# A Fourier mixing layer rebuilt inside a fused fp32 kernel: tiles by row quarter, a ring of weights, four column tiles

## The chip, the cores and the metric

One core of a Trainium2 chip runs the whole program. The metric is the device time of one execution in microseconds. The profile is of one such execution; all times in it count from the first instruction.

## What is computed

The input x has shape (8, 32, 32, 192) in fp32. Two layers follow one another; the change is in the first and in where things lie.

```python
def layer0(x, w1, b1, ...):
    xn = layernorm(x, norm1_w, norm1_b)
    xf = rfft2(xn, axes=(1, 2), norm='ortho')        # 32 x 17 bins
    xf = xf.reshape(B, h, w // 2 + 1, 8, 24)
    o1 = einsum('bhwni,hwnio->bhwno', xf, w1c) + b1c # own weights in every bin
    o1 = complex(relu(o1.real), relu(o1.imag))
    xs = irfft2(o1, s=(h, w), axes=(1, 2), norm='ortho')
    xm = layernorm(xs, norm2_w, norm2_b)
    return xs + x + gelu(xm @ mlp_w1 + mlp_b1) @ mlp_w2 + mlp_b2
def layer1(x, ...):                                  # not touched but for buffers
    h = gated_scan(layernorm(x), 8 steps)
    x = x + h
    return x + gelu(layernorm(x) @ mlp_w1 + mlp_b1) @ mlp_w2 + mlp_b2
```

## The kernel before

`build` (L202) runs `fourier` (L216), `inverse_rows` (L703), `mlp` (L818) for the first layer, then `gated_scan` (L1137) and `mlp` again. Each function opens a block with one program per engine; the programs wait on semaphores, and the order on each engine is the order in which it is written. SP, ACT and POOL also issue DMAs, each in its own program: while an engine issues, what is behind waits.

**Row stage (in `fourier`).** X (64 tiles of 128 tokens by 192 channels; a tile is four image rows) is loaded by POOL, one image of 8 tiles at a time (L357). Per image DVE takes the statistics (L483, L489, with an epsilon added at L491), ACT the root, and DVE (L506) and ACT (L409) normalise four tiles each into `row_bufs`. PE multiplies by the row DFT (L620), ACT copies PSUM out (L419), and SP stores the result into the DRAM tensor `rows_spectrum`, four DMAs per image (L304). POOL meanwhile clears S and Y with memsets (L365, L366), loads small vectors, and when all images are normalised adds the second MLP bias b2 to all 64 tiles of X (L375). ACT's program also issues the weights of the first two units between images (`load_weights`, L282/L283).

**Unit loop (in `fourier`).** The 17 column bins are taken in 8 groups g of two bins; each group has two halves s of 96 channels: 16 units, and two units more for the last (Nyquist) bin, which fill one bin each. Of a group, `d2` is loaded (SP, L315), and PE applies the DFT down the columns with the data as the loaded operand (L642; L652 for the Nyquist part that comes with group 0). DVE scales by the layernorm gain into `xh` (L535; for the group 0 the constant term is added at L544), ACT's or SP's queue expands `xh` by DMA into S, which holds each of the four 24-channel blocks in its own place with zeros elsewhere (`expand`, L291). The products (L667) take S as the loaded operand, 64 columns with a stride of 256 bytes, and the weights Wt as the streamed one, 48 wide, in two column tiles of the array; a matmul is two records in the profile. ACT copies cross terms (L449, L451), DVE adds (L564), transposes (L571) and applies the relu (L575) into Z. PE inverts the columns of a group (L677), DVE copies into `d3` (L584, L608), and POOL stores `d3` to the DRAM tensor `rows_mixed` (L382, L387).

**Inverse rows and the first MLP.** `inverse_rows` loads `rows_mixed` again (SP, L734), multiplies (L751), copies to XS (ACT, L766) and takes statistics (L785, L790), while ACT and POOL split the MLP weights into high and low parts (`high_parts`, `low_parts`, L806 to L815). In `mlp`, DVE scales XS into xn (L999), eight operations per group of four tiles, while POOL adds XS to X, 16 operations of four tiles (L905), signalled by the semaphore `biased`. In the second `mlp` POOL instead adds b2 tile by tile (L900).

## Time and profile before

| | us |
|---|---|
| median of 3 runs (1276.23 to 1278.8) | 1276.27 |
| the profiled execution | 1273.96 |
| its span, first to last instruction | 1272.6 |
| PE / DVE / ACT / POOL busy in it | 1114.9 / 879.9 / 665.2 / 347.9 |
| mean granted TensorE clock | 0.889 |

The span lies 1.4 us under the execution's own time, and that one 2.3 us under the median of the runs. Busy shares are averages over stages that have different limits: the Fourier layer takes the first 392 us, its MLP, the scan and the second MLP the rest.

### The profile page before, as it was taken

The page shows a single profiled execution, that of the slowest core. Times are in us where ns is not written, and L with a number is a line of the kernel's source. Part 1 is how long each engine was busy: PE and PEld are TensorE (multiplying, and loading weights), DVE is VectorE, ACT ScalarE, POOL GpSimd, SP SyncE. Part 2 cuts the span into 40 slices and gives each one's busy share as a digit, 9 for nine tenths or more (in the row PEclk, how much of TensorE's full clock was granted, in tenths as well). Part 3 has the DMA queues.
Part 4 walks back from the last instruction along what each step waited for, and adds up shares of the span by engine and source line. Part 5 has one row for each costly group of instructions (what it writes and reads, how often), then busy time and mean ns, then how long its engine had stood idle before and what let it go on. Part 6 is the DMA issues. An engine that isn't in the chain of part 4 may idle for free. (4 is left out here: it accounts for less than half of the span.)

```text
span 1272.6 us, 22506 instructions
## 1 busy us (share of the span) xinstructions
PE 1114.9 (88%) x7072; PEld 905.8 (71%) x7072; DVE 879.9 (69%) x2183; ACT 665.2 (52%) x1299; POOL 347.9 (27%) x351
## 2 busy tenths in 40 slices
PE   2634799999754899999989999999999889999998
PEld 1224788888522788888876776767767668889997
DVE  6626465555437788887776877969969867766665
ACT  2421334344133565666667757756664346676555
POOL 4564011001008200000013743734716621111110
PEclk9665677878567899999999999999999879999999
DMA  8653999996172000000010000000000000001001
GB/s 245 146 133 76 178 174 201 198 182 122 31 202 65 1 1 0 0 0 0 0 44 1 1 1 1 1 1 1 1 1 1 1 1 25 25 26 36 25 25 37
DMA packets 153073, 70.22 MB, mean 55 GB/s; under 512 B 117968, under 2 KB 145392, under 8 KB 153008
## 3 DMA queue, kind: packets, MB, share of 16 engines
q1 hardware_dynamic: 129208, 47.38, 18.2%
q10 hardware_dynamic: 19232, 9.18, 3.8%
q0 software_dynamic: 4576, 12.93, 3.5%
q8 instruction: 33, 0.54, 0.2%
q14 instruction: 24, 0.20, 0.1%
HBM read 43.91 MB, written 18.87 MB: 49 GB/s over the span
## 5 line engine op out<-in xcount | busy, mean ns | idle before, releaser
L1129 PE MATMUL L_conv_ps<-w2hl,L_conv_hhi 128*128 128x384 f32 x768 | 229.0, 366 | 1.3 <-DVE X L1025 1.3
L939 ACT ACTIVATE L_conv_hf<-L_conv_ps,L_conv_b 128x512 f32<-128x512 f32 x192 | 132.1, 688 | 175.0 <-PE L_conv_ps L1110 170.2
L1129 PE MATMUL L_conv_ps<-w2hl,L_conv_hlo 128*128 128x192 f32 x768 | 188.6, 252 | 0.0
L1015 DVE TENSOR_TENSOR L_conv_hlo<-L_conv_hf,L_conv_hhi 128x512 fp32r<-128x512 f32 x192 | 129.4, 688 | 84.5 <-ACT L_conv_hhi L948 81.5
L1521 PE MATMUL sc_ps<-sc_hi,wh 128*128 128x512 f32 (+1 forms) x440 | 161.0, 438 | 3.4 <-ACT sc_prod L1303 3.2
L1129 PEld LDWEIGHTS L_conv_ps<-w2hl,L_conv_hhi 128*128 128x128 f32 x768 | 144.7, 188 | 4.6 <-DVE X L1025 2.1
L1521 PE MATMUL sc_ps<-sc_hi,wl 128*128 128x512 f32 (+1 forms) x440 | 147.8, 392 | 0.0
L1129 PEld LDWEIGHTS L_conv_ps<-w2hl,L_conv_hlo 128*128 128x128 f32 x768 | 146.6, 191 | 0.0
L449 ACT ACTIVATE cross<-psF 32x192 f32<-32x192 f32 x136 | 43.8, 322 | 175.1 <-PE psF L667 165.9
L1376 DVE TENSOR_TENSOR sc_prod<-sc_ps,sc_gate 128x512 f32<-128x512 f32 x168 | 110.2, 680 | 15.1 <-PE sc_ps L1521 15.1
L948 ACT ACTIVATE L_conv_hhi<-L_conv_hf 128x512 fp32r<-128x512 f32 x192 | 116.3, 622 | 0.0
L1521 PEld LDWEIGHTS sc_ps<-sc_hi,wh 128*128 128x128 f32 (+1 forms) x440 | 70.7, 187 | 55.2 <-issue 40.0
L1521 PE MATMUL sc_ps<-sc_lo,wh 128*128 128x512 f32 (+1 forms) x440 | 107.6, 393 | 0.0
L1243 POOL TENSOR_TENSOR sc_lo<-sc_prod,sc_hi 128x512 fp32r<-128x512 f32 x64 | 95.2, 1511 | 22.7 <-ACT sc_hi L1319 22.7
L900 POOL TENSOR_TENSOR X<-X,L_conv_b 128x192 f32 x64 | 36.8, 606 | 193.8 <-DVE L_conv_xn L999 193.8
L642 PE MATMUL psF<-fwd_h,d 128*96 128x128 f32 x256 | 56.3, 410 | 36.9 <-DVE dc L552 18.7
L564 DVE TENSOR_TENSOR Y<-psF,cross 128x192 f32<-128x192 f32 (+1 forms) x72 | 25.6, 356 | 87.1 <-ACT cross L451 87.1
L1110 PE MATMUL L_conv_ps<-L_conv_thi,w1h 128*128 128x512 f32 x192 | 77.8, 405 | 7.0 <-ACT L_conv_hf L939 4.2
L1521 PEld LDWEIGHTS sc_ps<-sc_lo,wh 128*128 128x128 f32 (+1 forms) x440 | 71.2, 188 | 15.2
L1110 PE MATMUL L_conv_ps<-L_conv_tst,w1h 128*128 128x512 f32 x192 | 77.2, 402 | 2.5 <-DVE L_conv_tst L1010 2.5
L642 PEld LDWEIGHTS psF<-fwd_h,d 128*96 128x96 f32 x256 | 51.7, 269 | 38.9 <-DVE dc L552 18.9
L1521 PEld LDWEIGHTS sc_ps<-sc_hi,wl 128*128 128x128 f32 (+1 forms) x440 | 71.0, 188 | 10.3
(139 smaller groups left out, 2313.8 us busy)
## 6 DMA issues: line engine op xcount, KB each, us to landing
row_bufs<-in_L_conv_w SPq DMA_DIRECT2D x16, 576.0 KB
Wt<-in_L_conv_w SPq DMA_DIRECT2D x14, 576.0 KB
X<-in_x POOLq DMA_DIRECT2D x8, 768.0 KB, 6.0
rows_spectrum<-row_bufs SPq DMA_DIRECT2D x32, 192.0 KB, 3.3
d<-rows_spectrum SPq DMA_DIRECT2D x8, 768.0 KB, 4.9
S<-xh ACTq DMA_DIRECT2D x64, 96.0 KB
rows_mixed<-d POOLq DMA_DIRECT2D x32, 192.0 KB, 5.9
d<-rows_mixed SPq DMA_DIRECT2D x8, 768.0 KB, 8.5
```

The costliest lines, as they stand in the source:

```text
L449: nc.scalar.activation(cross[j % 2][re:re + H], v[im:im + H, :, :, 1], ACT.Copy, scale=-1.0).then_inc(crossed, 1)
L564: nc.vector.tensor_tensor(Y[0:n, 8 * j:8 * j + 8, :], v[0:n, :, :, 0], cross[j % 2][0:n], ALU.add).then_inc(summed, 1)
L642: mm = pe.matmul(ps[0:HALF, 4 + q, P * b:P * b + P], d2[:, 4 * q + b, HALF * s:HALF * s + HALF], table, start=True, stop=True)
L900: nc.gpsimd.tensor_tensor(X[:, GT * i + k, :], X[:, GT * i + k, :], b2[:, :], ALU.add).then_inc(biased, 1)
L939: nc.scalar.activation(hf[:, m % 3, :], ps[:, RB + m % 2, :], gelu, bias=b1[:, m:m + 1]).then_inc(act1, 1)
L948: nc.scalar.activation(hhi[:, m, :], hf[:, m % 3, :], ACT.Copy).then_inc(h_hi, 1)
L1015: nc.vector.tensor_tensor(hlo[:, m, :], hf[:, m % 3, :], hhi[:, m, :].bitcast(F32), ALU.subtract).then_inc(h_lo, 1)
L1110: mm = pe.matmul(ps[:, RB + m % 2, :], w, x[:, :], start=(q == 0), stop=(q == 4))
L1129: mm = pe.matmul(o, x, w, start=(m == 0 and n == 0), stop=(m == MT - 1 and n == 1), skip_group_check=True)
L1243: nc.gpsimd.tensor_tensor(lo[c][:, j, :], value(c, s)[:, j, :], hi[c][:, j, :].bitcast(F32), ALU.subtract).then_inc(q["h_lo"], 1)
L1376: step_product = nc.vector.tensor_tensor(prod[c][:, j, :], ps[:, 3 * c + j, :], gate[c][:, j, :], ALU.mult)
L1521: return pe.matmul(out, ww[rows, cols], x[rows, j, :], start=first, stop=last, skip_group_check=True)
```

## The change

- Tiles are numbered by row quarter: eight slabs, each with one group of four rows of each of the 8 images, in place of eight images. Slabs of x, normalised x and row spectra live in XS, which is now there from the start. X is not filled in the row stage.
- `rows_spectrum` is laid out so that a slab is stored by one DMA of rows of 6144 bytes, on POOL (L366). The memsets on POOL and the 64 additions there go; the additions now stand in the loop of POOL in the first `mlp` (L837), ahead of the wide addition (L842), with a wait on the new semaphore `based` between them.
- The weights go through a ring of four units in X's place, all issued by SP, from the third slab on. After the last four units SP loads x once more into X (`again`), and the MLP weights.
- A unit has both bins of one half, and the Nyquist bin with both halves is one unit (`None`): 17 units. In the products (L621) the weights are the loaded operand, 24 columns in each of four column tiles, and S streams, 64 wide at a stride of 256 bytes; real and imaginary weights accumulate, so S has three parts (-im, re, im).
- S is written from PSUM directly: for every part and channel block one scaling by gain times mask, 12 on DVE (first four images) and 12 on ACT (other four). `xh`, the expansion DMAs, the cross copies and the sums go.
- ACT applies the relu from PSUM (two of 512 elements a unit) into Y, DVE transposes 1024 elements into Z.
- The inverse column transform (L637) goes in halves between the units. `d3` is copied by DVE and ACT and written into XS by DMAs within SBUF (POOL, L374, 8 per group, 96 KB each); `rows_mixed` and its loads are gone, and `inverse_rows` works in place.
- The scan's buffers move into XS, and the output is stored slab by slab.

The core of the diff:

```diff
-        F1 = nc.dram_tensor("rows_spectrum", [W, H, B, C], F32, kind="Internal").ap()
-        F2 = nc.dram_tensor("rows_mixed", [B, H, W, C], F32, kind="Internal").ap()
+        F1 = nc.dram_tensor("rows_spectrum", [P, TPB, B * C], F32, kind="Internal").ap()
...
+        Wt = [X[0:HALF + NH, NT // RING * r:NT // RING * (r + 1), :].rearrange("p a c -> p (a c)").rearrange(
+            "p (k h o r) -> p k h o r", k=2, h=H, o=BS) for r in range(RING)]
...
+        units = [(0, 0), (0, 1), None] + [(g, s) for g in range(1, NG) for s in range(2)]
...
         @block.sync
+            sp.wait_ge(x_in[XT - 1], 16)
+            for u in range(UNITS):
+                r = u % RING
+                if u >= RING:
+                    sp.wait_ge(mixed, 2 * (u - RING + 1))
+                for k in range(2):
+                    s, at = (k, WF - 1) if units[u] is None else (units[u][1], 2 * units[u][0] + k)
+                    into = Wt[r][:, k].rearrange("p h o r -> p h (o r)")
+                    sp.dma_start(into[0:HALF], w_v[s, at]).then_inc(w_in[r], 16)
+                    sp.dma_start(into[HALF:HALF + NH], b_v[s, at]).then_inc(w_in[r], 16)
...
+            for u in range(UNITS - RING, UNITS):
+                sp.wait_ge(mixed, 2 * (u + 1))
...
+                again(u)
...
         @block.gpsimd
-            for s in range(2):
-                nc.gpsimd.memset(S[s][:, :, :], 0.0).then_inc(zeroed, 1)
-            nc.gpsimd.memset(Y[:, :, :], 0.0).then_inc(zeroed, 1)
...
-            with pool.Fori(0, B) as b:
-                for k in range(TPB):
-                    nc.gpsimd.tensor_tensor(X[:, b * TPB + k, :], X[:, b * TPB + k, :], sh.b2["L0_conv_"][:, :],
-                                            ALU.add).then_inc(x_biased, 1)
...
+            for k in range(TPB):
+                if k + XT < TPB:
+                    load(k + XT)
+                pool.wait_ge(d1_done, 4 * (k + 1))
+                pool.dma_start(F1[:, k, :], d1[k % 2].rearrange("p b c -> p (b c)")).then_inc(f1_out[k % 2], 16)
...
+            for g in range(NG):
+                pool.wait_ge(d3_v, 2 * (g + 1))
+                pool.wait_ge(d3_a, 2 * (g + 1))
+                for k in range(TPB):
+                    pool.dma_start(XS[g:P:NG, B * k:B * (k + 1), :].rearrange("p b c -> p (b c)"),
+                                   d3[g % 2][k:P:TPB, :]).then_inc(sh.rows_in[g % 2][k], 16)
...
         @block.vector
+            def spread(u):
+                dve.wait_ge(hdft, u + 1)
+                if u >= 2:
+                    dve.wait_ge(mixed, 2 * (u - 1))
+                v = ps[0:HALF, col_bank(u), :].rearrange("p (b r f) -> p r b f", b=B // 2, r=2)
+                for cut, of in slots(u):
+                    for part, n in itertools.product(range(3), range(NH)):
+                        scale = (ngm if part == 0 else gm)[:, of, n:n + 1]
+                        nc.vector.tensor_scalar(S[u % 2][0:HALF, part, n, 0:B // 2, cut], v[:, int(part != 1), :, cut], scale,
+                                                None, ALU.mult).then_inc(spread_v, 1)
...
         @block.tensor
-            def products(u, s, g, p, times, bins=2):
-                for j in range(4):
-                    passed(pe, summed, 4 * (u - 1) + j + 1)
-                    for hl in range(8):
-                        for k in range(bins):
-                            h = 8 * j + hl
-                            mm = pe.matmul(ps[2 * H * k:2 * H * k + 2 * H, j, 48 * hl:48 * hl + 48],
-                                           S[s][:, :, k * H + h], Wt[p][s][:, k, h, :], start=True, stop=True)
+            def products(u):
+                r = u % RING
+                pe.wait_ge(w_in[r], 64 * (u // RING + 1))
+                spread_done(u)
+                for hl in range(H // 2):
+                    q, col = hl // 8, 2 * NH * B * (hl % 8)
+                    if hl % 8 == 0 and u >= 2:
+                        pe.wait_ge(relu, 2 * (u - 2) + q + 1)
+                    for part in range(2):
+                        for j in range(4):
+                            k, h = j // 2, H // 2 * (j % 2) + hl
+                            mm = pe.matmul(ps[H * j:H * j + BS, 2 * (u % 2) + q, col:col + 2 * NH * B],
+                                           Wt[r][:, k, h, :, part],
+                                           S[u % 2][:, 1 - part:3 - part, :, :, k * H + h].rearrange("p a n b -> p (a n b)"),
+                                           start=(part == 0), stop=(part == 1), skip_group_check=True)
...
+                for k in range(GT):
+                    nc.gpsimd.tensor_tensor(X[:, GT * i + k, :], X[:, GT * i + k, :], b2[:, :],
+                                            ALU.add).then_inc(biased if XS is None else based, 1)
+                if XS is not None:
+                    pool.wait_ge(based, GT * (i + 1))
                     tiles = bass.ds(GT * i, GT)
                     nc.gpsimd.tensor_tensor(X[:, tiles, :], X[:, tiles, :], XS[:, tiles, :], ALU.add).then_inc(biased, GT)
```

How the order moves on PE in the unit loop. Before, units run in a loop over pairs of groups, with the products of one unit in four quarters, then the columns of the unit two ahead, then in every second unit a whole inverse:

```order
L667 MATMUL psF<-Wt,S 64x48 x16
L78 REGISTER_ALU
L667 MATMUL psF<-Wt,S 64x48 x16
L78 REGISTER_ALU
L667 MATMUL psF<-Wt,S 64x48 x16
L78 REGISTER_ALU
L667 MATMUL psF<-Wt,S 64x48 x16
L633 ISA
L640 ISA
L642 MATMUL psF<-fwd_h,d 96x128 x4
L640 REGISTER_ALU
L642 MATMUL psF<-fwd_h,d 96x128 x4
```

Of the changed kernel, the same place, written out without a loop (`spectrum` is S, `X` holds the ring of weights):

```order
L621 MATMUL psF<-spectrum,X 24x64 x128
L604 MATMUL psF<-fwd_h,d 96x128 x8
L637 MATMUL psF<-Z,inv_h 128x384 x2
L621 MATMUL psF<-spectrum,X 24x64 x128
L604 MATMUL psF<-fwd_h,d 96x128 x8
L637 MATMUL psF<-Z,inv_h 128x384 x2
```

A unit has 128 product matmuls where it had 64, and two inverse matmuls stand behind every unit where four stood behind every second one.

On POOL at the start of the first MLP, before:

```order
L891 MEMSET raw 128x320
L892 MEMSET raw 128x256
L907 UNCONDITIONAL_BRANCH
L907 ISA
L905 TENSOR_TENSOR X<-X,XS 128x768
```

And in the changed kernel, where the last rows are the loop's body:

```order
L829 MEMSET spectrum 128x320
L830 MEMSET spectrum 128x256
L848 UNCONDITIONAL_BRANCH
L848 ISA
L837 TENSOR_TENSOR X<-X,L_conv_b 128x192
L837 ISA
L837 TENSOR_TENSOR X<-X,L_conv_b 128x192
L837 ISA
L837 TENSOR_TENSOR X<-X,L_conv_b 128x192
L837 ISA
L837 TENSOR_TENSOR X<-X,L_conv_b 128x192
L840 ISA
```

The four bias additions now stand ahead of each wide addition, and the ISA row of L840 is the wait on `based`.

## Rows read from the trace of the kernel before

**Rows 1.** The page: engines (busy us, share, instructions), and a DMA issue (median us).

```profile
PE 1114.9 (88%) x7072; PEld 905.8 (71%) x7072; DVE 879.9 (69%) x2183; ACT 665.2 (52%) x1299; POOL 347.9 (27%) x351
...
rows_mixed<-d POOLq DMA_DIRECT2D x32, 192.0 KB, 5.9
```

**Rows 2.** Stretches of core 0: engine busy us (instructions), PEclk, DMA share, GB/s.

```profile
77.00:118.00 41.00, 11.24 (x68) 11.00 (x68) 24.18 (x15) 0.00 (x0) 33.19 (x61) 0.58 0.22 55
118.00:342.00 224.00, 207.16 (x2464) 187.40 (x2462) 114.95 (x193) 86.91 (x271) 21.83 (x31) 0.72 0.92 163
```

**Rows 3.** Timeline, row stage: start us, us, engine, line, operation, [idle before <-releaser].

```profile
15.90 6.25 PE L620 MATMUL psF<-row_bufs,fwd_w 128*128 128x384 f32 x12 [15.90 <-DVE row_bufs L506]
...
26.75 6.19 DVE L491 TENSOR_SCALAR mvb<-mvb 128x8 f32<-128x8 f32 x1
...
37.81 1.86 ACT L409 ACTIVATE row_bufs<-X,shift,rs 128x192 f32 x4 [13.08 <-issue]
...
61.22 0.32 ACTq L282 DMA_DIRECT2D Wt<-in_L_conv_w  x1
...
68.25 1.86 ACT L409 ACTIVATE row_bufs<-X,shift,rs 128x192 f32<-128x192 f32 x4 [6.68 <-issue]
```

**Rows 4.** Timeline between the last row copy and the first products.

```profile
76.71 2.69 SPq L304 DMA_DIRECT2D rows_spectrum<-row_bufs  x4
...
85.47 6.68 POOL L375 TENSOR_TENSOR X<-X,L_conv_b 128x192 f32 x12
...
87.07 3.70 PE L642 MATMUL psF<-fwd_h,d 128*96 128x128 f32 x16 [10.91 <-DMA d<-rows_spectrum]
...
91.78 18.75 DVE L544 TENSOR_SCALAR xh<-xh,dc 96x8 f32<-96x8 f32 x1
...
117.81 7.35 PE L667 MATMUL psF<-Wt,S 100*64 100x48 f32 x128 [0.97 <-DVE x L549]
```

**Rows 5.** Timeline, the unit loop: two starts of products a group apart, one single-tile unit.

```profile
212.29 7.37 PE L667 MATMUL psF<-row_bufs,S 100*64 100x48 f32 x128
...
236.75 0.43 PE L667 MATMUL psF<-Wt,S 100*64 100x48 f32 x4
...
327.49 14.39 PE L667 MATMUL psF<-Wt,S 100*64 100x48 f32 x128
```

**Rows 6.** Products line L667 alone, in two stretches at different granted clock.

```profile
119.30:124.30 5.00, 5.00 (x96) 5.00 (x94) 0.50 1.10 248
...
223.00:228.00 5.00, 5.00 (x96) 5.00 (x92) 1.00 0.94 235
```

**Rows 7.** Groups by shape in 118 to 342 us: count, busy us, mean ns, idle before.

```profile
L642 PE MATMUL psF<-fwd_h,d 128*96 128x128 f32 x224 | 48.9, 408 | 7.3 <-DMA d<-rows_spectrum 7.3
...
L449 ACT ACTIVATE cross<-psF 32x192 f32<-32x192 f32 x136 | 43.8, 322 | 175.1 <-PE psF L667 165.9 <-issue 7.0
...
L571 DVE STREAM_TRANSPOSE Yt<-Y 128x768 f32<-128x768 f32 x17 | 35.2, 2073 | 0.1
L677 PE MATMUL psF<-Z,inv_h 128*128 128x384 f32 x64 | 29.4, 593 | 9.4 <-DVE Z L575 4.8 <-DVE d L584 4.6
L535 DVE TENSOR_SCALAR xh<-psF,gamma 96x256 f32<-96x256 f32 x56 | 24.0, 475 | 12.6 <-PE psF L642 12.5
```

**Rows 8.** Timeline, the last products and the inverse row transform.

```profile
341.91 0.32 ACT L449 ACTIVATE cross<-psF 32x192 f32<-32x192 f32 x1 [1.10 <-PE psF L667]
...
366.00 1.65 PE L751 MATMUL psI<-d,inv_w 128*128 128x384 f32 x2 [14.69 <-DMA d<-rows_mixed]
```

**Rows 9.** Timeline, the start of the first MLP: POOL and DVE.

```profile
392.70 29.35 POOL L905 TENSOR_TENSOR X<-X,XS  x16
...
393.22 13.70 DVE L999 TENSOR_SCALAR L_conv_xn<-XS,mv,L_conv_rs 128x192 f32<-128x192 f32 x8
...
413.20 9.71 DVE L999 TENSOR_SCALAR L_conv_xn<-XS,mv,L_conv_rs 128x192 f32<-128x192 f32 x8
...
431.95 2.15 DVE L999 TENSOR_SCALAR L_conv_xn<-XS,mv,L_conv_rs 128x192 f32<-128x192 f32 x8
```

More of the change, by code:

```diff
@@ new lines, in fourier, with operations, slots @@
+        UNITS = len(units)
+        last_of = [2] + [2 * g + 2 for g in range(1, NG)]
+        def operations(u, engine):
+            halves = 2 if units[u] is None else 1
+            return 3 * NH * halves + (NH if u < 2 and engine == "v" else 0)
+        spread_by = {e: list(itertools.accumulate(operations(u, e) for u in range(UNITS))) for e in "va"}
+        def slots(u):
+            if units[u] is None:
+                return [(slice(H * s, H * (s + 1)), s) for s in range(2)]
+            return [(slice(0, 2 * H), units[u][1])]
@@ L610, in _ @@
+            inverse_out(NG - 2, 1) if last_of[NG - 2] + 2 >= UNITS else None
+            for half in range(2):
+                inverse_out(NG - 1, half)
         @block.tensor
@@ L671, in inverse @@
-            def inverse(g, rows=P, width=P):
-                pe.wait_ge(relu, 2 * (g + 1))
-                z = Z[0:rows].rearrange("p b s c -> p (b s c)")
-                for j in range(4):
-                    passed(pe, d3_done, 4 * g + j - 1)
-                    pe.matmul(ps[0:width, 6 + j % 2, 0:384], inv_h[0:rows, 0:width], z[:, 384 * j:384 * j + 384],
-                              start=True, stop=True).then_inc(inv_done, 1)
-            def group(g, p, times):
-                for s in range(2):
-                    products(2 * g + s, s, g, p, times)
-                    if not (isinstance(g, int) and g == NG - 1):
-                        columns(2 * (g + 1) + s, s, g + 1)
-                    if s == 0 and not (isinstance(g, int) and g == 0):
-                        inverse(g - 1)
@@ L689, in _, with spread_done @@
[L689 to L703 removed]
+            def spread_done(u):
+                pe.wait_ge(spread_v, spread_by["v"][u])
+                pe.wait_ge(spread_a, spread_by["a"][u])
@@ new lines, in _ @@
+            pe.wait_ge(d1_done, 4 * TPB)
+            pe.wait_ge(consts, 16 * 3)
+            columns(0)
+            columns(1)
+            for u in range(UNITS):
+                products(u)
+                if u + 2 < UNITS:
+                    columns(u + 2)
+                for g in range(NG):
+                    if u == last_of[g] + 1:
+                        inverse(g, 0)
+                    elif u == last_of[g] + 2:
+                        inverse(g, 1)
+            inverse(NG - 2, 1) if last_of[NG - 2] + 2 >= UNITS else None
@@ L706, in inverse_rows @@
+            for half in range(2):
+                inverse(NG - 1, half)
+def inverse_rows(nc, t, sh, XS):
     mv = sh.mv
```

673 lines of the change are left out of this document (293 added, 380 removed).

## The prediction

> **What bounds the kernel now.** I read the engine table of the page first: TensorE (PE) is busy 88% of the span [rows 1], but from 437 us on it runs without a hole, and the change leaves that part alone. So I cut the first 437 us into stages with the busy times by stretch [rows 2]. Two things stand out. From 77 to 118 us PE does 11.2 us of work in 41, and POOL is the engine that is full (33.2). From 118 to 342 us PE is busy 207 of 224 us at a mean granted clock of 0.72, with the DMA engines at 0.92 beside it. Then I read the timeline of each stage for what ended last. In the row stage two waits stop everything: the DVE row of 6.19 us beside POOL's memsets, and ACT's two idle times of 13.08 and 6.68 us ended by "issue", during which ACT only issues weight loads [rows 3]. Between the stages the columns start 10.4 us after the last row copy, through two DMA legs, and then one tiny DVE addition lasts 18.75 us while POOL runs its additions X += b2 at 0.557 us each (6.68/12) [rows 4]. In the loop one group of two units takes 24.46 us (212.29 to 236.75), so 12.2 per unit, of which products take 7.37 [rows 5]. After it the inverse row transform waits 14.69 us for a store and a load [rows 8], and the first MLP starts slowly beside POOL [rows 9].
>
> **Row stage and hand-over.** The weight loads leave ACT's queue for SP's, and the POOL memsets go (one DVE memset of PSUM instead). An undisturbed stretch is 37.81 to 61.22 us, four images, 5.85 each, 5.95 with the steps between [rows 3]. First matmul at 15.9 as before, eight tiles: 15.9 + 8 x 5.95 = 63.5, last copy about 64 instead of 76.7. Four units of weights are now loaded in that stage beside X and F1; SP's other work is small, and POOL's queue carries X loads and F1 stores, each of the latter waiting for its tile, which holds back only loads three tiles ahead. I cost that at nothing, and bound it by 0 and 8 us (if the DMA engines are as full as in the loop, 0.92 and more). To the columns 11 us (10.4 before): 75. Columns 3.7. Then DVE and ACT each scale 12 pieces of 96x256 from PSUM. DVE's nearest row is 0.475 us for the same shape [rows 7], a little less back to back, 12 x 0.43 = 5.2; ACT's nearest is 0.322 for 192 elements [rows 7], so 12 x 0.4 = 4.8 beside it. Four additions of the DC term and hand-overs take 1.8. First products at 75 + 3.7 + 5.2 + 1.8 = **85.8 against 117.8: minus 32.0**. The largest part is the removed wait of 18.75 behind POOL and the expansion DMAs behind it.
>
> **Unit loop.** A unit now has 128 matmuls instead of 64, in four column tiles of 24 columns instead of two of 64, and the 64-wide operand with a stride of 256 B streams instead of being loaded. What does one cost? In two tiles 128 records take 7.37 us. The single-bin unit uses one tile and takes 14.39 for 128 records, 112 ns each [rows 5]; so each tile goes at 112 ns per record and two do not disturb one another. The same unit runs at one speed at granted clock 0.50 and 1.00 (96 records in 5.00 us in both) [rows 6], so the pace is not the array's but of reading or issuing. My value: four tiles at 112 ns side by side, 256/4 x 112 = 7.17, plus 0.2 for waits: P = 7.36, as before. Bounds: below, 6.4, if loading 24 columns instead of 64 shortens a record by some 15%; above, 14.4, if only two tiles advance at once. I take the value in the row's own manner because both pieces of a record stay about as large together. 17 x 7.36 = 125. Columns cost 48.9/14 = 3.5 per unit, 15 of them: 52. Inverse: 29.4/64 x 4 = 1.85 per half, 14 halves: 26 [rows 7]. The additions of group 0 and the Nyquist columns: 4. Sum 207, so the last products end at 85.8 + 207 = **293 against 342: 49 us ahead, 17 more than at the start**. The old loop had 18 units, of which two were single-tile at 14.39; they are one unit of 7.36 now, which saves 21.4, and the rest (group 0 inside the loop, one more pass of columns) gives some 4 back.
>
> What hides in it: DVE per unit transposes 1024 elements instead of 768 (2.07 x 4/3 = 2.76), scales 12 pieces (4.8) and copies (0.5): 8.1 us of 12.4. ACT: two rectifications of 512 elements (about 0.7 each), 12 scalings (4.8), a copy: 6.7. The next columns need the previous spread, which is through 8.3 us after its products end, while the next-but-one column pass comes 12.6 after. The expansion DMAs go, so DMA (0.92 with them) falls. None of them becomes late unless a scaling takes over 0.75 us.
>
> PE instruction overhead: the Trainium skill, "TensorEngine Tiling (Array Packing)", section Instruction Overhead, says a matmul has some 60 cycles of its own and that no tiling should be taken from a side that is already small. By it, as an estimate, 256 records of 25 to 50 ns, issued one by one, would take 6.4 to 12.8 us, so it speaks for the slow side of this term; the trace, with 57.5 ns per record in two tiles and 112 in one, does not show the floor.
>
> **Tail.** Before, 24.1 us from the last products to the inverse rows: turn, inverse, and 14.69 of two DMA legs [rows 8]. Now one leg on the same POOL queue, 5.9 us from issue to landing [rows 1], 6.3 with its first issue: 24.1 - 8.4 = 15.7. The inverse rows keep their 26 us (same matmuls, same copies, in place). MLP start at 293 + 41.7 = **334.7 against 392.1: minus 57.4**. The reload of X (8 x 768 KB) begins four units before the end and its last quarter lands some 10 us after the products, under the 42 us; cover gone, it would cost the difference.
>
> **First MLP.** The 64 additions X += b2 don't go away; they now stand in POOL's loop there. Before, 16 additions of 768 elements take 29.35 us, and DVE's scalings crawl beside them: 8 in 13.70, 8 in 9.71, the next 8 free in 2.15 [rows 9]. So one DVE operation passes per POOL operation of 1.8. Now an iteration is 4 x 0.557 + 0.2 + 1.83 = 4.3 us, the burst 16 x 4.3 = 69 instead of 29. How many DVE operations pass per iteration? The row of 18.75 us [rows 4] says that between additions which follow without a wait none gets in (18.75/0.557, some 34 in a row). A gap comes where POOL waits for its four additions, and after the wide one: two. So 8 scalings take 17.4, three groups 52 instead of 25.6; a little of it is covered: **plus 24**. Bounds: minus 5, if one passes after each addition (three groups in 21), and plus 47, if only one gets in per iteration (two groups in 70, the third in 2.2).
>
> The Trainium skill, "SBUF — State Buffer", section Who interferes with whom, calls this an exclusive lock on the port pair shared by DVE and GpSimd, held for one instruction; by it DVE would get in at the end of each addition and the term would be minus 5 instead of plus 24. The row of 18.75 us through 34 additions speaks against it.
>
> **Sum.** 1273.96 (the profiled execution) - 57.4 + 24 = 1240.6. The median of the runs before is 2.3 above the profiled execution; added, **1243 us** against 1276.27, 33 us or 2.6% faster. A change under 0.2% (2.5 us) is what a measurement of this kernel can't tell from none.
>
> **Rivals.**
> (A) *Slower: the four tiles advance in pairs only*, or the strided stream takes twice what the strided load took. The place is the products of every unit, the price 17 x (14.4 - 7.36) = 120 us: 1243 + 120 = 1363. It decides from P = 9.3 on (33/17 above 7.36), where the whole gain is gone. For it: the clock-independent 57.5 ns per record [rows 6], which fits a limit shared by both tiles as well as one of each; against it, the 112 ns of a lone tile [rows 5]. Chance 0.17.
> (B) *A floor of issuing or reading near 36 ns per record*, between the two: P = 9.2, 17 x 1.84 = 31 more: 1274, about the time before. For it the page named above; nothing in the rows. Chance 0.11, split over the bound on both sides.
> (C) *POOL's additions let DVE in each time*: term minus 5, so 1214. Chance 0.08, for the rule of the lock, against it the 18.75 us. Its opposite, one slot per iteration, gives 1266 and lies within the forecast's range.
> (D) *Products faster*, P = 6.4: 17 x 0.96 = 16 less, 1227. The loaded side shrinks from 64 to 24 columns. Chance 0.12.
> (E) *The change doesn't do what it says*: the spread from PSUM costs over 0.75 us a piece, and DVE paces the unit at 14 us: 17 x 1.7 = 29 more, 1272. Against it 0.475 for the same shape. Chance 0.04.
> Forecast: 0.48, its own range 1228 to 1266.
>
> **How the numbers follow.** Below 1212 I leave 0.04, above 1308 0.16 (rival A in full). Range **1212 to 1308**. Faster: forecast 0.48 + C 0.08 + D 0.12 + 0.02 of E and 0.04 of B = 0.74, less 0.03 for the row stage's and MLP's upper bounds falling together: 0.71. Same: 0.04. Slower: 0.25.
>
> **What would show it.** In the changed profile: first products at 86 us; 256 records of products in 7.4 us per unit (this is the step that could be wrong by most; over 9.3 and the kernel is not faster); unit period 12.4; last products at 293; MLP start at 335; the first scalings of that MLP in 17 us per eight, and POOL's burst of 69 us. A first-products time over 94 would say that the four units of weights crowd the row stage. A DVE row of 17 us anywhere before the loop would say a POOL operation was left there.

## The result and the profile after

| | before | changed |
|---|---|---|
| median of 4 runs each, us | 1276.25 (1274.5 to 1278.8) | 1227.14 (1223.21 to 1229.31) |
| the profiled execution / its span | 1273.96 / 1272.6 | 1229.31 / 1227.1 |
| first products / last products end | 117.8 / 342 | 90.0 / 303.0 |
| inverse rows start / first MLP starts | 366.0 / 392.1 | 323.8 / 347.4 |

The changed kernel takes 0.961 of the time before (95% interval 0.9581 to 0.964): 3.9%, 49 us faster. The profiled execution of the changed kernel was its longest of the four, 2.2 us over the median.

The two profiled spans differ by 45.5 us. By the table, 27.8 of them lie before the first products, 11 between these and the end of the last products, 3.3 from there to the inverse rows, 2.5 in the inverse rows and 1.2 in the first MLP.

From the page of the changed kernel, the engines and the queue that loads program code (packets, MB, share of 16 DMA engines; before it had 33 packets and 0.54 MB):

```profile
PE 1092.4 (89%) x9256; PEld 885.9 (72%) x9256; DVE 854.0 (70%) x2230; ACT 697.0 (57%) x1293; POOL 365.5 (30%) x388
...
q8 instruction: 55, 0.90, 0.3%
```

Busy time by stretch (length, then PE, PEld, DVE, ACT, POOL busy with counts, granted clock, DMA share, GB/s), to hold against [rows 2]:

```profile
77.00:90.00 13.00, 5.92 (x36) 5.77 (x37) 5.55 (x17) 5.60 (x16) 9.18 (x17) 0.63 0.48 138
90.00:303.00 213.00, 192.82 (x4677) 173.54 (x4677) 103.89 (x237) 110.81 (x247) 22.82 (x48) 0.87 0.82 151
303.00:324.00 21.00, 5.06 (x14) 2.38 (x14) 2.80 (x4) 2.50 (x4) 7.58 (x16) 0.74 0.63 150
324.00:347.00 23.00, 22.48 (x64) 12.80 (x64) 17.99 (x110) 17.20 (x36) 6.17 (x3) 0.93 0.01 1
347.00:420.00 73.00, 56.24 (x278) 46.78 (x279) 66.81 (x132) 33.63 (x59) 70.25 (x75) 0.88 0.04 9
```

The empty stretch before the loop is 13 us of columns and spread instead of 41. In the loop (90 to 303) PE is busy 193 of 213 us, where it was 207 of 224, at a mean granted clock of 0.87 instead of 0.72.

The timeline around it. DVE waits for a slab of x, the last row copies, the first columns, the first unit of products; before, the last row copy began at 76.2 and the products at 117.81 [rows 4]:

```profile
17.60 0.36 DVE L479 BATCH_NORM_STATS2 st<-XS 128x6 f32<-128x192 f32 x1 [5.26 <-issue]
...
67.14 1.60 ACT L402 ACTIVATE XS<-psF 128x384 f32<-128x384 f32 x4
...
80.60 5.90 PE L604 MATMUL psF<-fwd_h,d 128*96 128x128 f32 x32 [12.40 <-DMA d<-rows_spectrum]
...
89.97 7.43 PE L621 MATMUL psF<-spectrum,X 100*24 100x64 f32 x256 [3.48 <-ACT spectrum L431]
```

Groups by shape in the loop (count | busy us, mean ns | idle before, releaser), which answer to [rows 7]:

```profile
L621 PE MATMUL psF<-spectrum,X 100*24 100x64 f32 x4352 | 129.5, 290 | 23.7 <-issue 20.2 <-ACT spectrum L431 3.5
...
L604 PE MATMUL psF<-fwd_h,d 128*96 128x128 f32 x224 | 40.3, 354 | 0.0
...
L439 ACT ACTIVATE Y<-psF 128x512 f32<-128x512 f32 x33 | 34.7, 1052 | 69.3 <-PE psF L621 69.3
...
L545 DVE STREAM_TRANSPOSE Z<-Y 128x1024 f32<-128x1024 f32 x15 | 18.7, 1246 | 85.4 <-ACT Y L439 85.4
```

The products' idle time of 23.7 us, 20.2 of it ended by "issue", is new. Its place shows on PE's timeline of 199 to 217 us:

```profile
199.00 2.19 PE L621 MATMUL psF<-spectrum,X 100*24 100x64 f32 x70 [1.01 <-issue]
201.13 3.65 PE L604 MATMUL psF<-fwd_h,d 128*96 128x128 f32 x16
204.61 1.46 PE L637 MATMUL psF<-Z,inv_h 128*128 128x384 f32 x4
206.00 4.88 PE L621 MATMUL psF<-spectrum,X 100*24 100x64 f32 x164
213.56 2.87 PE L621 MATMUL psF<-spectrum,X 100*24 100x64 f32 x92 [2.69 <-issue]
```

PE stops at 199.00 and again at 213.56, in the middle of a unit's products both times, and between the stops stand 70 + 16 + 4 + 164 = 254 matmul records. I went through the 12 stops of over 0.7 us within units: from one to the next it is 254 or 255 records (seven times), or two or two and a half times as many (509, 637), whatever the matmuls are. No data has that period. The half steps mean that the period is 127 records, of which these stops mostly take every second.

The tail, against [rows 8]:

```profile
302.93 1.84 PE L637 MATMUL psF<-Z,inv_h 128*128 128x384 f32 x4
...
303.05 1.03 ACT L439 ACTIVATE Y<-psF 128x512 f32<-128x512 f32 x1 [5.00 <-PE psF L621]
...
310.11 3.79 POOL L374 DMA_DIRECT2D XS<-d  x8 [0.23 <-issue]
...
323.80 2.90 PE L695 MATMUL psI<-XS,inv_w 128*128 128x384 f32 x4 [14.77 <-PEq L244]
```

And the start of the first MLP on POOL and DVE, against [rows 9]:

```profile
347.98 2.24 POOL L837 TENSOR_TENSOR X<-X,L_conv_b 128x192 f32 x4
350.40 1.82 POOL L842 TENSOR_TENSOR X<-X,XS  x1 [0.18 <-POOL X L837]
...
348.50 5.44 DVE L940 TENSOR_SCALAR L_conv_xn<-XS,mv,L_conv_rs 128x192 f32<-128x192 f32 x8
...
358.55 5.32 DVE L940 TENSOR_SCALAR L_conv_xn<-XS,mv,L_conv_rs 128x192 f32<-128x192 f32 x8
...
374.19 5.36 DVE L940 TENSOR_SCALAR L_conv_xn<-XS,mv,L_conv_rs 128x192 f32<-128x192 f32 x8
```

Eight scalings take 5.4 us beside POOL's narrow additions with one wide one among them, where they took 13.70 and 9.71 beside the wide ones alone. From the MLP's start to the scan's first transposes it is 270.5 us (347.4 to 617.9) against 271.7 before (392.1 to 663.8).

### The profile page after: what moved, and what is told of

Same layout as the page of the kernel before. It is cut to its first block and busy times, and to the rows that moved or that the text cites. A ratio compares the mean times of both kernels' runs of the same rounds, so it can differ in the third digit from the quotient of the medians.

```text
span 1227.1 us, 26088 instructions
## 1 busy us (share of the span) xinstructions
PE 1092.4 (89%) x9256; PEld 885.9 (72%) x9256; DVE 854.0 (70%) x2230; ACT 697.0 (57%) x1293; POOL 365.5 (30%) x388
## 5 line engine op out<-in xcount | busy, mean ns | idle before, releaser
L956 DVE TENSOR_TENSOR L_conv_hlo<-L_conv_hf,L_conv_hhi 128x512 fp32r<-128x512 f32 x192 | 141.3, 751 | 78.1 <-ACT L_conv_hhi L889 75.4
L1185 POOL TENSOR_TENSOR sc_lo<-XS,sc_hi 128x512 fp32r<-128x512 f32 x96 | 142.8, 1503 | 116.4 <-ACT sc_hi L1261 116.4
L621 PE MATMUL psF<-spectrum,X 100*24 100x64 f32 x4352 | 129.5, 290 | 23.7 <-issue 20.2
L621 PEld LDWEIGHTS psF<-spectrum,X 100*24 100x24 f32 x4352 | 121.6, 122 | 34.9 <-issue 34.7
L837 POOL TENSOR_TENSOR X<-X,L_conv_b 128x192 f32 x128 | 83.1, 680 | 194.2 <-DVE L_conv_xn L940 194.2
L1261 ACT ACTIVATE sc_hi<-XS 128x512 fp32r<-128x512 f32 x144 | 88.0, 631 | 83.7 <-DVE XS L1326 27.6
L1318 DVE TENSOR_TENSOR XS<-sc_ps,XS 128x512 f32<-128x512 f32 x168 | 110.1, 680 | 14.6 <-PE sc_ps L1463 14.5
L374 POOL DMA_DIRECT2D XS<-d x64 | 30.4, 483 | 197.3 <-DVE d L554 197.1
L545 DVE STREAM_TRANSPOSE Z<-Y 128x1024 f32<-128x1024 f32 x16 | 19.9, 1246 | 96.3 <-ACT Y L439 96.3
```

The source lines that it names most:

```text
L374: pool.dma_start(XS[g:P:NG, B * k:B * (k + 1), :].rearrange("p b c -> p (b c)"), d3[g % 2][k:P:TPB, :]).then_inc(sh.rows_in[g % 2][k], 16)
L621: mm = pe.matmul(ps[H * j:H * j + BS, 2 * (u % 2) + q, col:col + 2 * NH * B], Wt[r][:, k, h, :, part], S[u % 2][:, 1 - part:3 - part, :, : ...
L837: nc.gpsimd.tensor_tensor(X[:, GT * i + k, :], X[:, GT * i + k, :], b2[:, :], ALU.add).then_inc(biased if XS is None else based, 1)
L956: nc.vector.tensor_tensor(hlo[:, m, :], hf[:, m % 3, :], hhi[:, m, :].bitcast(F32), ALU.subtract).then_inc(h_lo, 1)
L1185: nc.gpsimd.tensor_tensor(lo[c][:, j, :], value(c, s)[:, j, :], hi[c][:, j, :].bitcast(F32), ALU.subtract).then_inc(q["h_lo"], 1)
L1261: nc.scalar.activation(hi[c][:, j, :], value(c, s)[:, j, :], ACT.Copy).then_inc(q["h_hi"], 1)
```

## The experiments

Each stands against the changed kernel (1227.14, profiled 1229.31), or, those named b, against the kernel before. A single time has a scatter of some 3 us either way. The kernel before, run again beside them, had medians of 1274.0 to 1274.9, 1.4 to 2.2 us under the 1276.25 above, so that a median lower by as much is no gain.

**Is the pace of the products one of the tiles, of the order, or of the strided stream?** Three kernels, one execution each. The first streams adjacent elements:

```diff
-                                           S[u % 2][:, 1 - part:3 - part, :, :, k * H + h].rearrange("p a n b -> p (a n b)"),
+                                           spectrum[u % 2][0:HALF + NH, 2 * NH * B * (k * H + h):2 * NH * B * (k * H + h + 1)],
```

The second keeps the two parts of a tile together, and the third uses two tiles:

```diff
-                    for part in range(2):
-                        for j in range(4):
+                    for j in range(4):
+                        for part in range(2):
```

```diff
-                            mm = pe.matmul(ps[H * j:H * j + BS, 2 * (u % 2) + q, col:col + 2 * NH * B],
+                            mm = pe.matmul(ps[H * (j % 2):H * (j % 2) + BS, 2 * (u % 2) + q, col:col + 2 * NH * B],
```

> The changed kernel, but the streamed operand of the products is read as 64 adjacent elements instead of 64 at a stride of 256 bytes (so the products are of other data). Theory T (what I forecast with): each tile goes at 112 ns a record because of what one record reads, whichever side is strided; then the stretch of 256 records falls clearly below 7.4 us, to some 5 us or less. Rival I: one record is issued every 29 ns whatever it reads; then it stays at 7.4 us.

Measured: 1217.25 us. Its PE timeline, and the group of all products:

```profile
92.57 5.40 PE L621 MATMUL psF<-spectrum,X 100*24 100x64 f32 x256 [3.93 <-ACT spectrum L431]
...
100.77 3.25 PE L621 MATMUL psF<-spectrum,X 100*24 100x64 f32 x217
...
L621 PE MATMUL psF<-spectrum,X 100*24 100x64 f32 x4352 | 79.0, 235 | 56.7 <-issue 52.6 <-ACT spectrum L431 3.9
```

The first unit takes 5.40 us for 256 records, in part at the low clock. Of the second, 217 records take 3.25 us, 15 ns each. Over the loop the starts of records lie 14.0 ns apart (median over runs of 8 records) against 28.1 in the changed kernel. So at the full clock the stride doubles the price of a product. The products alone, in a stretch at the low clock and in one at the full clock:

```profile
93.60:96.60 3.00, 3.00 (x124) 3.00 (x118) 0.50 0.02 5
...
226.60:228.20 1.60, 1.60 (x118) 1.60 (x122) 1.00 1.33 196
```

With the adjacent stream the pace follows the clock: the median spacing is 26.7 ns at a granted clock of 0.50 (1.2 GHz) and 13.9 at 1.00 (2.4 GHz), while with the strided one it is 28.1 at both. At the low clock the adjacent stream gains next to nothing. The idle time ended by "issue" grew from 20.2 to 52.6 us.

> The changed kernel, but both accumulating matmuls of a tile stand next to each other (tile, then part) instead of going round the four tiles twice. Theory T, tiles side by side with a short queue between them: 256 records stay within 10% of 7.4 us. Rival: only neighbours in the instruction stream overlap, so pairs on one tile run one behind the other and 256 records take 10 to 14 us.

Measured: 1226.64 us. A whole unit of it:

```profile
217.35 7.41 PE L621 MATMUL psF<-spectrum,X 100*24 100x64 f32 x256
```

7.41 us for 256 records: the order of the tiles made no difference.

> The changed kernel, but the 256 records of a unit go to two column tiles instead of four (the other two quarters of the output stay zero). Theory T (112 ns per record and tile): 14.4 us per unit, 17 x 7 = 119 us longer as a whole. Rival I (29 ns per record from issuing, not from tiles): 7.4 us per unit as now and no change of the time.

Measured: 1312.04 us.

```profile
108.78 14.39 PE L621 MATMUL psF<-spectrum,X 100*24 100x64 f32 x256
...
L621 PE MATMUL psF<-spectrum,X 100*24 100x64 f32 x4352 | 244.7, 288 | 3.9 <-ACT spectrum L431 3.9
```

14.39 us for the same 256 records: 112 ns per record in each of two tiles, as in the lone tile of before [rows 5] and in each of the four (28.1 x 4). So with a strided operand the pace belongs to the tile, and up to four tiles don't slow one another. The whole is 85 us longer, not 119, because PE's stops are gone (none within a unit, against 23 us) and the columns run at a higher clock (277 ns each instead of 354; the granted clock is 1.00 from 96 to 384 us).

**What are the stops?** Two kernels. The first fills the ring of weights once:

```diff
-            for u in range(UNITS):
+            for u in range(RING):
                 r = u % RING
-                if u >= RING:
-                    sp.wait_ge(mixed, 2 * (u - RING + 1))
...
-                pe.wait_ge(w_in[r], 64 * (u // RING + 1))
+                pe.wait_ge(w_in[r], 64)
```

The second makes a loop of PE's units 5 to 12 (`unit` holds a unit's products, columns and inverse, and its waits grow with i):

```diff
-            for u in range(UNITS):
-                products(u)
...
+            FIRST, TIMES = 5, 2
+            for u in range(FIRST):
+                unit(u)
+            with pe.Fori(0, TIMES) as i:
+                for u in range(FIRST, FIRST + RING):
+                    unit(u, i)
+            for u in range(FIRST + RING * TIMES, UNITS):
+                unit(u)
```

> The changed kernel, but the ring of weights is filled once and never again (units from the fifth on use the weights of the first four). In the changed kernel PE stops 12 times in the middle of products for 0.7 to 3.5 us, always a multiple of 254 to 255 records apart, 20 us in all. Theory F (each stop is a load of the next 16 KB of PE's program, which comes late because the weights fill the DMA engines): with the weight traffic gone the stops fall below 5 us in all and the last products end 15 to 20 us earlier. Rival W: the stops are waits for weights or for the relu, or the program load is slow by itself: they stay, 15 us or more (for the relu or the program) while only a weight wait would go too, which would leave no spacing of 254.

Measured: 1202.02 us. Its loop, 93 to 276 us:

```profile
93.00:276.00 183.00, 177.90 (x4673) 162.49 (x4665) 102.76 (x236) 110.73 (x246) 22.80 (x48) 0.96 0.28 86
```

The stops within units fell from 12 with 23.3 us to 4 with 6.2 us, at places of the same series (three of them exactly as in the changed kernel). The loop is 183 us long instead of 213: 17 us from the stops, and most of the rest from faster columns (mean 297 ns instead of 354) at a granted clock of 0.96 instead of 0.87. Theory F holds: most of the stops go with the weight traffic. How far they scatter by themselves is seen where nothing of it was changed: 18.9 us in e2 and 18.6 in the execution of e4 that was profiled.

The trace of the changed kernel shows the loads themselves. The queue for program code moves 36 packets of 16384 bytes in the loop:

```profile
q8 instruction: 36, 0.59, 1.3%
```

One comes for every 127 records of PE (first to last stop: 32 packets, 4071 records), and every stop, the thirteenth of 0.3 us too, ends 1.3 to 1.7 us after such a packet has landed; so does each of the four stops of e5 (1.3 to 1.4). Why a load comes late beside the weights isn't shown: once under way, a packet takes 1.21 us in the changed kernel and 1.10 in e5.

A stop costs twice, once itself and once in the clock that PE is granted after it. In the loop of the changed kernel the granted clock falls from 1.00 to 0.50 eleven times, each time 0.8 to 3.8 us after PE went idle in one of these stops. In e3, without a stop, it doesn't fall from 96 us to the end of the loop.

> The changed kernel with PE's units 5 to 12 as a loop of four units run twice, all other engines as they are. Theory F1 (stops are first-time loads of PE's program, and a body of four units stays with the engine): in units 9 to 12 no stops, about 5 us less in all. Theory F2 (a body of four units, some 1100 records, is too long to stay): stops as before and no change of the time within 3 us. Rival W (stops are data waits): no change either, but the spacing of 254 records goes on without regard to the loop's ends.

Measured: median 1227.25 (1225.45 to 1231.63), no change. Its second pass begins at 204 us and stops as before:

```profile
210.91 3.77 PE L621 MATMUL psF<-spectrum,X 100*24 100x64 f32 x127 [3.06 <-issue]
...
226.11 1.07 PE L621 MATMUL psF<-spectrum,X 100*24 100x64 f32 x31 [0.75 <-issue]
...
238.73 1.76 PE L621 MATMUL psF<-spectrum,X 100*24 100x64 f32 x54 [2.41 <-issue]
```

22.6 us of stops in all, and two code packets more than the changed kernel (57 against 55). F2 holds: a loop whose body is these four units loads its code again on each pass. Had the body stayed, its 1104 records would have saved some 8 packets. Rival W, waits for data, falls with it: from the last stop of the first pass to the first of the second it is 220 records, no multiple of 127. The Trainium skill, "Runtime: NRT & Kernel Launch", section Instruction fetch mechanics, says that program is streamed in blocks of 256 instructions through the engine's own DMA queue, the cost being mostly hidden. The packets of 0.90/55 = 0.016 MB agree, and so does the period, since 127 records with their 127 weight loads make 254 instructions, and a few waits. Hidden the cost was fully only where the engine was slow: no stops at 14.4 us per 256 records (e3), 23 us at 7.2, 57 us at 3.6 (e1).

**Do the weights crowd the row stage?**

```diff
-            sp.wait_ge(x_in[XT - 1], 16)
+            sp.wait_ge(x_in[(TPB - 1) % XT], 16 * ((TPB - 1) // XT + 1))
```

> The changed kernel, but SP starts to load weights only when the last of the eight slabs of x has landed, not after the third. In the row stage DVE waits 19 us for slabs. Theory: the weights crowd out x, so the last row copy comes near 64 us instead of 68.7; first products then 3 to 5 us earlier than 90.0, if unit 0's weights (1.2 MB, 8 us) are there by then; but the ring is behind by four units, DMA at some 9 us per unit against 12, so the loop loses up to 5 us in its first units. Net between minus 5 and plus 5 us. Rival: slabs come no earlier (their own latency sets it): no change in the row stage, and a few us slower.

Measured: median 1224.40 (1222.72 to 1225.42); ratio to the kernel before 0.9606 (0.9582 to 0.963), which overlaps the changed kernel's. The median is 2.7 us lower, but the kernel before, run beside it, was 2.2 us lower too: no gain in the whole can be told.

```profile
62.30 1.64 ACT L402 ACTIVATE XS<-psF 128x384 f32<-128x384 f32 x4
...
77.18 5.27 PE L604 MATMUL psF<-fwd_h,d 128*96 128x128 f32 x32 [13.85 <-DMA d<-rows_spectrum]
```

The last row copies come 4.8 us earlier (62.30 against 67.14), the columns at 77.18 against 80.60. The other profiles bear this out: the last row copy ends at 63.9 and 63.8 where the weights start late (here and in v2), and at 67.8 to 73.5 in the eight where they don't. So the delay in the row stage is the weights' doing. Part of it comes back: from the last copy to the columns it is 13.2 us instead of 11.9, with SP's loads now in that stretch. The last products end 5.7 us earlier than in the changed kernel.

**What do POOL's additions cost the MLP?**

```diff
-                for k in range(GT):
-                    nc.gpsimd.tensor_tensor(X[:, GT * i + k, :], X[:, GT * i + k, :], b2[:, :],
-                                            ALU.add).then_inc(biased if XS is None else based, 1)
+                if XS is None:
+                    for k in range(GT):
+                        nc.gpsimd.tensor_tensor(X[:, GT * i + k, :], X[:, GT * i + k, :], b2[:, :],
+                                                ALU.add).then_inc(biased, 1)
                 if XS is not None:
-                    pool.wait_ge(based, GT * (i + 1))
```

> The changed kernel without POOL's 64 additions of b2 at the start of the first MLP (the bias is left out of the result). I had costed them at plus 24 us; the trace shows the MLP 1.2 us shorter than before with them. Theory L (one DVE operation gets in at the end of every POOL addition, so they cost next to nothing): DVE scalings of 8 take 10 to 14 us again as in the kernel before, since they now meet only the wide additions, and the time is within 5 us of the changed kernel, possibly longer at the start. Rival: the additions do delay the MLP and something else paid for it: the time falls by 10 us or more.

Measured: median 1226.91 (1224.22 to 1229.33). The scalings and POOL's burst without the additions:

```profile
347.45 13.70 DVE L940 TENSOR_SCALAR L_conv_xn<-XS,mv,L_conv_rs 128x192 f32<-128x192 f32 x8
...
367.43 9.71 DVE L940 TENSOR_SCALAR L_conv_xn<-XS,mv,L_conv_rs 128x192 f32<-128x192 f32 x8
...
346.93 29.35 POOL L842 TENSOR_TENSOR X<-X,XS  x16
```

The rows of before are back to the hundredth (13.70, 9.71), and the time is the same. The whole MLP, to the scan's first transposes, takes 272.0 us without the additions and 270.5 with them. So the additions make DVE wait less per operation but for a longer time (POOL's burst is 80 us, 347.98 to 428.24, instead of 29), and both cancel. Theory L holds.

**Why did the small addition wait 18.75 us, when the scalings don't?** Three forms of line L544 in the kernel before, each in place of the line removed in the first cut: eight adjacent elements (b1), 192 adjacent elements (b2), and 192 with subtract and multiply by two scalars, the scalings' own form (b3).

```diff
-                nc.vector.tensor_scalar(xh[s][:, 0, :, 0], xh[s][:, 0, :, 0], dc[:, s:s + 1], None,
+                nc.vector.tensor_scalar(xh[s][:, 0, 0, 0:B], xh[s][:, 0, 0, 0:B], dc[:, s:s + 1], None,
```

```diff
+                nc.vector.tensor_scalar(xh[s][:, 0, 0:3, :], xh[s][:, 0, 0:3, :], dc[:, s:s + 1], None,
```

```diff
+                nc.vector.tensor_scalar(xh[s][:, 0, 0:3, :], xh[s][:, 0, 0:3, :], dc[:, s:s + 1], gamma[:, s:s + 1],
+                                        ALU.subtract, ALU.mult).then_inc(xh_done, 4)
```

> The kernel before, but its small DVE addition of 96x8 elements, which lasted 18.75 us beside POOL's additions, works on eight adjacent elements instead of eight at a stride of 256 bytes (so the constant term is added in the wrong place). Theory: what keeps DVE out is that a tiny or strided operation loses every hand-over to POOL; if the stride is what matters, the row falls to below 1 us and the time by some 18 us. Rival: the form does not matter and POOL's loop with no wait in it does: the row stays at 18 us and more.

Measured: 1275.73 us, the row 19.15 us.

> The kernel before, but its small DVE addition beside POOL's additions takes 192 adjacent elements instead of 8 (it adds the constant term in places where it doesn't belong). Theory: the size decides who gets in; the row then lasts 0.6 to 1.2 us and the time falls by some 15 us. Rival: size does not matter either, the row stays at 17 us and more, and the cause of the 18.75 us stays open.

Measured: 1276.21 us, the row 19.18 us.

> The kernel before, with the DVE operation beside POOL's additions in the form of the scalings of the MLP (192 adjacent elements, subtract and multiply with two scalars by partition) in place of one addition; its result is not the constant term's. Stride and size did not matter (rows of 19.15 and 19.18 us). Theory: the form decides, as scalings of this form do get in after every addition in the MLP; the row lasts 0.6 to 1.2 us. Rival: the form doesn't matter either, the row stays at 17 us or more, and the difference lies in what surrounds the two places.

Measured: 1279.21 us (the kernel before beside it: 1275.89).

```profile
93.43 18.66 DVE L544 TENSOR_SCALAR xh<-xh,dc,gamma 96x192 f32<-96x192 f32 x1
```

All three theories of mine fell. Neither stride, size nor form lets the operation in; it waits in each case to the end of POOL's run. DVE as such isn't shut out: beside the same additions, just before this row, four scalings that read PSUM run freely, two of them here in the kernel before:

```profile
90.81 0.87 DVE L535 TENSOR_SCALAR xh<-psF,gamma 96x256 f32<-96x256 f32 x2 [0.83 <-PE psF L642]
```

Two things differ from the MLP. There eight scalings follow one another and the first starts 0.5 us after POOL's first addition, while here one operation comes 16 to 17 us into a run of 64; and there the scaling reads one tile and writes another, while all forms here read and write the same. I tried neither, and the cause stays open.

**Can both gains be had?** The layout of S is the thing to change: the frequency outermost, so that a product streams adjacent elements. v1 does that, v2 starts the weights late as well, with the edit of e6.

```diff
-    s = np.zeros((HALF + NH, 3, NH, B, 2 * H))
+    s = np.zeros((HALF + NH, 2 * H, 3, NH, B))
     for n in range(NH):
-        s[HALF + n, 1, n] = 1
+        s[HALF + n, :, 1, n] = 1
...
-        S = [spectrum[k][0:HALF + NH, :].rearrange("p (a n b f) -> p a n b f", a=3, n=NH, b=B) for k in range(2)]
+        S = [spectrum[k][0:HALF + NH, :].rearrange("p (f a n b) -> p a n b f", a=3, n=NH, b=B) for k in range(2)]
```

> The changed kernel with S laid out so that the 64 elements that a product streams are adjacent (the frequency index outermost); DVE and ACT then write S at a stride of 384 bytes. With adjacent data of other content a record took 14.0 ns instead of 28.1, but PE's stops grew from 23 to 57 us and the time fell by 10 to 12 us. Theory S (the stride of the streamed operand sets P, and writing with a stride is free): products at 14 ns again, time 1215 to 1219. Rival: the price moves to the writers: a scaling goes from 0.40 us spacing to 0.8 and more on DVE or ACT, 12 of them outlast the unit, and the time is the same or longer.

Measured: median 1219.88 (1218.32 to 1220.37), 0.9574 of the kernel before (0.9547 to 0.96). Its groups in the loop:

```profile
L621 PE MATMUL psF<-spectrum,X 100*24 100x64 f32 x4350 | 80.5, 238 | 55.7 <-issue 51.9 <-DVE spectrum L534 3.8
...
L431 ACT ACTIVATE spectrum<-psF,gm 96x256 f32<-96x256 f32 x123 | 61.1, 724 | 0.0
...
L528 DVE TENSOR_SCALAR spectrum<-psF,ngm 96x256 f32<-96x256 f32 x60 | 31.5, 641 | 9.7 <-PE psF L604 9.7
```

Records at 14.0 ns, stops at 55.9 us in 18 places. The writers pay: ACT's scaling 724 ns instead of 467 to 497, DVE's 641 instead of 469. They still fit in the loop (DVE 121 of 194 us, ACT 130). Ahead of it the price shows: from the first columns to the first products it is 10.4 us instead of 9.4. So writing with a stride isn't free, as I had put it, but mostly hidden, and the time lies just above the 1215 to 1219 that I expected.

> The same layout, and the weights' loading begins only after the last slab of x. If both gains are real and independent (10 to 12 and 2 to 5 us): 1210 to 1216. If the faster loop makes the ring of weights the bound, the late start costs what it gains and the time is that of the layout alone.

Measured: median 1219.33 (1213.68 to 1225.09), 0.957 (0.9541 to 0.9599). Its profiled execution, at 1213.9, has the first products at 87.2 and 54.6 us of stops; over six runs it can't be told from v1, and the median misses the 1210 to 1216 of two added gains: the time is that of the layout alone. By the medians both beat the changed kernel by 7 to 8 us, by the ratios to the kernel before beside them by some 5, and the intervals of the ratios overlap a little with the changed kernel's; they beat the kernel before by 54 to 55. Undisturbed and at the full clock PE now does a unit's products in 3.8 us (the unit at 211.4 us in v1), and then waits for its own program.

## Why the prediction was right, and where its sizes were off

I forecast 1243 in a range of 1212 to 1308, faster with 0.71; it is 1227. The total is off by 16 us: the gain is half as much again as forecast. It lies just outside the 1228 to 1266 of the forecast proper and on the 1227 of rival D, but not by D's mechanism, for the products were no faster. Several steps missed in opposite directions. So it is in part luck that the total came out closer than the term of the first MLP:

| step | forecast | measured |
|---|---|---|
| last row copy ends | 64 | 68.7 |
| first products | 85.8 | 90.0 |
| products of a unit, undisturbed | 7.36 | 7.4 |
| first products to end of last | 207 | 213 |
| last products to inverse rows | 15.7 | 20.8 |
| inverse rows to MLP start | 26 | 23.6 |
| term of the first MLP | +24 | -1.2 |
| profiled execution | 1240.6 | 1229.3 |

*The row stage.* "I cost that at nothing" was the wrong end of its own bound of 0 to 8: the four units of weights cost 4.8 us (e6). The sum could have shown it: the DMA share in the loop, with weights going, was already 0.92. The sign that I gave for it, first products over 94, was too coarse: they came at 90.0.

*The products.* The step that I called the riskiest held: 7.43 us for the first unit. e3 shows the premise (112 ns per record and tile, tiles apart from one another), so rival A's condition, pairs only, is false. But my reason for keeping 112 ns, that "both pieces of a record stay about as large together", wasn't the cause. e1 shows 56 ns per record and tile with an adjacent stream at the full clock: in the changed kernel the strided side sets the pace. Before, the strided side was the loaded one, also 64 elements at 256 bytes, and the pace was the same 112 ns at either clock; that the stride set it there too fits, but no run took it away. If so, that the pace stayed was luck: I had kept the stride without counting on it. Rival A's other half, that a strided stream takes twice what the strided load took, is false: both take 112 ns. The Trainium skill, "SBUF — State Buffer", section Door 1: The DMA port swizzle, says that accesses leaving a 16-byte line pay; 28.1 against 14.0 ns agrees in direction, and had I weighed it I would have seen the gain that v1 then took. Rival B (a floor near 36 ns) is refuted by 14.0 ns. The Trainium skill, "TensorEngine Tiling (Array Packing)", section Instruction Overhead, gives some 60 cycles per matmul, as an estimate 25 ns at 2.4 GHz. In four tiles records follow one another at 14.0 ns, so that there it doesn't show.

*The loop.* The pace was right, the sum 6 us too short, since some 23 us of waiting for program code were in no term; cheaper columns (40.3/14 = 2.9 us a unit instead of 3.5) and inverses (555 ns each instead of 593), at the higher clock, gave much of it back. Spread and transposes didn't bind: a transpose of 1024 elements took 1.25 us, where I had scaled 768 elements in 2.07 up to 2.76; before, it read Y at a stride, now adjacent elements, which may be why (not tried by itself).

*The tail.* I took one DMA leg of 6.3 us for two. Turn, inverse and copies took 7.1 us to the first of the last eight issues (310.11), 2.3 less than the sum has, but from there to the inverse rows it is 13.7 us, 7.4 more. The eight issues take 3.2 us to the point where POOL goes on. Then the end of the block (L244), at which all programs meet, waits for POOL:

```profile
L244 POOLq DRAIN  x1: 10083/10083/10083, 313.3 to 313.3; - x1
```

POOL's DRAIN ends at 323.37, and the inverse rows start at 323.80. The last of the eight DMAs had landed by 318.8, so what I had costed, the landing, isn't what ended last. e5, without reloads ahead of it, has a DRAIN of 9.93 us, so it isn't the weights'. The kernel before had one there too, of 5.2 us, and it stood between the store and the load of its two legs. Why the DRAIN outlasts the landing is open.

*The first MLP.* This is the step that failed: it alone is 25 us off, against some 13 us the other way in all steps before it. I let the one row of 18.75 us say that nothing passes between additions that follow without a wait, and gave rival C, the exclusive lock held for one instruction, only 0.08. One scaling passed per addition, as that rule says: eight took 5.4 us and not 17.4. POOL's burst was even longer than forecast, 80 us and not 69, and cost nothing: e4 shows the additions costing 0 within the scatter. My bound of minus 5 lay 4 us from the measured minus 1.2. The row on which I relied is real (b1 to b3 repeat it at 18.7 to 19.2 us), but it was no rule for this place.

## What to carry to other kernels

- A matmul's price can be that of one operand's stride. Measure one tile alone and several together, and try the operand adjacent before counting array cycles. Here a pace that ignored the clock (28.1 ns at both levels) was that of the strided stream; with the adjacent one the pace followed the clock (26.7 and 13.9 ns).
- Faster matmuls can bring the engine's own program onto the path. Here idle time ended by "issue", at multiples of a constant number of records, was code arriving late; the weights' traffic made it worse (23 us against 6), and a rolled loop with a body of some 1100 records didn't help.
- Where one block of programs hands over to the next, ask which engine reaches the end last and what it has to drain, not only when the data lands (323.4 against 318.8 us here).
- When one row sets a rule against another's evidence (here 18.75 us once against 16 scalings that got in one per POOL operation), give the second case its weight in chances, not only a bound.

## What the hardware showed that I had not expected

- PE stopped 12 times for over 0.7 us, 23 us in all, at multiples of 127 matmul records, each stop ending 1.3 to 1.7 us after a packet of program code had landed; 57 us with an adjacent stream, 6 without weight traffic, none with products at half the pace.
- Column tiles of 24 columns with a strided stream scale fully from two to four: a record every 55.5 ns in two, every 28.1 in four. In four with an adjacent stream it is 14.0 at the full clock.
- Beside POOL's additions of 0.56 us with one of 1.83 among them, eight DVE scalings take 5.4 us, beside those of 1.83 us alone 10 to 14 us, yet a single DVE operation in the kernel before waits 19 us through 34 additions in any form tried.
